# Second feed-forward product in three rounded-part products, in two halves of its inputs: a four-layer transformer stack on one Trainium2 core

## The reference, cut to what matters

```python
# each of blocks 0, 1, 2 (block 0 without the gate)
h = modulate(norm(x), cond)
q, k, v = h @ Wq + bq, h @ Wk + bk, h @ Wv + bv
x = x + gate1 * (softmax(q @ k.T * s) @ v @ Wp + bp)
h = modulate(norm(x), cond)
h = gelu(h @ W1 + b1, approximate=False)      # fc1: 256 -> 1024
x = x + gate2 * (h @ W2 + b2)                 # fc2: 1024 -> 256
# block 3: h2 = modulate(norm(h1)); return h2 + h1
```

## Time and profile before

| | |
|---|---|
| median of 3 runs | 1317.73 us (1311.64 to 1376.43) |
| profiled execution | 1313.94 us, of it 1312.2 us from first to last instruction |
| mean granted TensorE clock | 0.959 |
| TensorE matmuls busy | 1196.3 us |
| ScalarE busy | 777.1 us |
| VectorE busy | 780.6 us |
| GpSimd busy | 407.9 us |

### The profile page before, as it was taken

One profiled execution on the slowest core, in us unless ns is written; L12 is line 12 of the kernel. 1 busy time (PEld: TensorE's weight loads), 2 busy tenths in 40 slices (PEclk: granted clock), 3 DMA queues, 4 the chain that ended last, 5 costly groups with the idle time before them and its releaser, 6 DMA issues.

```text
span 1312.2 us, 19523 instructions
## 1 busy us (share of the span) xinstructions
PE 1196.3 (91%) x6484; PEld 725.4 (55%) x6484; DVE 780.6 (59%) x1587; ACT 777.1 (59%) x1363; POOL 407.9 (31%) x416
## 2 busy tenths in 40 slices
PE   4899998789989989999999989999999998999993
PEld 3668786445655545555555555556556555444432
DVE  4334245685685685574674654664755745787863
ACT  2563553267567468467566666575684674676771
POOL 2423255101143222332250251332322313434143
PEclk9999998799999999998999989999999999999987
DMA  7000000504304204312213331132133131242400
...
DMA packets 40852, 64.46 MB, mean 49 GB/s; under 512 B 11673, under 2 KB 26777, under 8 KB 40753
## 3 DMA queue, kind: packets, MB, share of 16 engines
...
## 4 chain that ended last, share of the span: by engine, by line
PE 67%; DVE 12%; issue 6%; SPq 6%; ACT 6%; DMA 2%; POOL 1%; ACTq 0%; POOLq 0%; DVEq 0%
PE ring L712 12%; PE ring L646 10%; PE AVB L659 9%; PE ring L572 8%; PE ring L574 7%; PE ring L573 7%; SPq L534 5%; PE ring L636 4%; DVE m L1049 4%; DVE stats L956 2%; PE ring L679 2%; PE ring L684 2%; ACT hT_h L762 1%; ACT L822 1%; ACT probs L822 1%
## 5 line engine op out<-in xcount | busy, mean ns | idle before, releaser
L1049 DVE TENSOR_REDUCE m<-ring 128x1 f32<-128x512 f32 x768 | 490.0, 684 | 181.7 <-PE ring L636 161.6
L822 ACT ACTIVATE probs<-ring 128x512 f32<-128x512 f32 x768 | 412.5, 612 | 265.2 <-PE ring L636 242.4
L646 PE MATMUL ring<-SQ,SK 49*128 49x512 f32 x768 | 292.4, 460 | 40.8 <-DVE cT L1056 15.0
L636 PE MATMUL ring<-SK,SQ 48*128 48x512 f32 x768 | 312.8, 477 | 16.6 <-ACT probs L822 13.5
L646 PEld LDWEIGHTS ring<-SQ,SK 49*128 49x128 f32 x768 | 131.7, 192 | 270.4 <-issue 90.3
L659 PE MATMUL AVB<-probs,V 128*32 128x512 f32 x1536 | 211.9, 620 | 0.8 <-issue 0.8
L712 PE MATMUL ring<-w_s,gT 128*128 128x256 f32 x768 | 176.8, 385 | 0.2
L636 PEld LDWEIGHTS ring<-SK,SQ 48*128 48x128 f32 x768 | 133.3, 193 | 55.5 <-ACT probs L822 40.4
L712 PEld LDWEIGHTS ring<-w_s,gT 128*128 128x128 f32 x768 | 143.3, 191 | 30.9 <-issue 12.2
L1158 POOL TENSOR_TENSOR tmp<-tmp,gates 128x256 f32<-128x256 f32 (+1 forms) x48 | 43.8, 914 | 253.0 <-DVE tmp L1097 217.7
L1126 POOL TENSOR_TENSOR postT_l<-full,postT_h 128x512 fp32r<-128x512 f32 x56 | 71.1, 1280 | 155.3 <-ACT postT_h L870 102.4
...
## 6 DMA issues: line engine op xcount, KB each, us to landing
...
gates<-gate_rows SPq DMA_DIRECT2D x12, 256.0 KB, 3.4
raw<-in_wqkv SPq DMA_DIRECT2D x9, 256.0 KB, 2.8
```

Of the source, the lines that this page charges most:

```text
L636: mm = pe.matmul(o[:, :], SQ[a % 4][r:r + KS, n // 2, c * P:(c + 1) * P], SK[a % 4][r:r + KS, n // 2, :], start=True, stop=True)
L646: mm = pe.matmul(o[:, :], SK[a % 4][r:r + KS + 1, n // 2, c * P:(c + 1) * P], SQ[a % 4][r:r + KS + 1, n // 2, :], start=True, stop=True)
L822: act.activation(probs[:, n % PROBS, :], bank(kind, a, i)[:, :], ACT.Exp, scale=SCALE[layer(unit_job(a))]).then_inc(done["scores"], 1)
L1049: nc.vector.tensor_reduce(m16[:, a % 2, col:col + 1], bank(kind, a, i)[:, :], AX_X, ALU.max, negate=True).then_inc(done["max"], 1)
```

## The change

- **fc2** becomes `product` of parts: `gT_h`, `gT_l` with `w2_h`, `w2_l`. `gelu` writes every hidden tile twice on ScalarE (`gT_f`, `gT_h`), and GpSimd subtracts (`gT_l`, in the same place as `gT_f`).
- To fit in memory `gT_h` and `gT_l` hold half of the hidden channels. So there is `fc2a` (the first 512 hidden channels) and `fc2` (the last 512), each as two steps of two token tiles; VectorE puts `fc2a` with the bias in `tmp` and adds `fc2` to it. The second gelu waits until `fc2a` has read the first half.
- The places: fc1 and gelu on ticks 8 and 13, `fc2a` on 11 and 12, `fc2` on 15 and on tick 0 of the next window, `v` for layers 2 and 3 on 9 and 10. In layer 0 `fc2a` comes after `pT0`, ahead of the second half of fc1.
- The second weight comes through `raw` in four pieces like the others. In layers 1 and 2 the nine pieces are split on every second tick from tick 8 of the layer's first window.
- `rowp` is loaded in a step of its own, `load_rows`, and the product with the gate rows is moved to `gatefix`, tick 4 of the next window. `wgate_s` is gone, its uses go through `wmod_s` and `qk`. The two-slot tile `full` is gone too: the full values lie where the remainder will be (`hT_f`, `postT_f`).

```diff
+T_FC1, T_FC2A, T_FC2 = (8, 13), (11, 12), (15, 16)
+T_V = (9, 10)
...
-        at[6] += [("v", j, 0), ("stack", UNITS * j, 0)]
-        at[7] += [("v", j, 1)]
+        at[6] += [("stack", UNITS * j, 0)]
+        at[T_V[0]] += [("v", j, 0)]
+        at[T_V[1]] += [("v", j, 1)]
...
-        for i, t in enumerate((8, 10)):
+        for i, t in enumerate(T_FC1):
             at[t] += [("fc1", j, m) for m in range(4 * i, 4 * i + 4)] + [("gelu", j, i)]
-        for t in range(TT):
-            at[12 + t] += [("fc2", j, t)]
+        for i in range(2):
+            at[T_FC2A[i]] += [("fc2a", j, i)]
+            at[T_FC2[i]] += [("fc2", j, i)]
     else:
+        at[4] += [("gatefix", j, 0)]
...
+def pieces_at(w):
+
+    first = TICKS * BATCH * layer(w)
+    if layer(w) == LAYERS - 1:
+        return [(first + 8, "wp", 0)]
+    order = [("wp", 0), ("w1", 0), ("w1", 1), ("w2", 0), ("w2", 1), ("w1", 2), ("w1", 3), ("w2", 2), ("w2", 3)]
+    return [(first + 8 + 2 * n, kind, i) for n, (kind, i) in enumerate(order)]
...
+        rest += [("split_" + kind, layer(w), i) for at, kind, i in pieces_at(w) if at == TICKS * w + t]
...
+        plan += [("load_" + kind, layer(w), i) for at, kind, i in pieces_at(w) if at == TICKS * w + t + 1]
         if t == 15 and batch(w) == 0:
-            plan.append(("load_wp", layer(w), 0))
...
+            plan.append(("load_rows", layer(w), 0))
...
-                elif kind == "fc2":
-                    pe.wait_ge(in_w2, 16 * (layer(a) + 1))
-                    for m in range(MT):
-                        if i == 0:
-                            pe.wait_ge(done["fc1"], nth("fc1", a, m))
-                        mm = pe.matmul(o[:, 0:DIM], gT[:, m, i * P:(i + 1) * P], w2_s[:, m, :],
-                                       start=(m == 0), stop=(m == MT - 1))
+                elif kind in ("fc2a", "fc2"):
+
+                    h = int(kind == "fc2")
+                    for t in range(2):
+                        tok = (2 * i + t) * P
+                        for m in range(MT // 2):
+                            if i == 0 and t == 0:
+                                pe.wait_ge(g_lo, (nth("gelu", a, h) - 1) * (MT // 2) + m + 1)
+                                pe.wait_ge(done["split_w2"], nth("split_w2", layer(a), 2 * h + m // 2))
+                            mm = product(o[:, t * DIM:(t + 1) * DIM], [x[:, m, tok:tok + P] for x in (gT_h, gT_l)],
+                                         [w[:, h * MT // 2 + m, :] for w in (w2_h, w2_l)], m == 0, m == MT // 2 - 1)
...
-                        act.activation(gT[:, m, :], bank("fc1", a, m)[:, :], ACT.Gelu,
-                                       bias=colv[:, layer(a), col:col + 1]).then_inc(done["fc1"], 1)
+                        for dst in (gT_f, gT_h):
+                            ins = act.activation(dst[:, m % (MT // 2), :], bank("fc1", a, m)[:, :], ACT.Gelu,
+                                                 bias=colv[:, layer(a), col:col + 1])
+                        ins.then_inc(done["fc1"], 1)
...
+                elif kind == "gelu":
+
+                    for m in range(MT // 2):
+                        pool.wait_ge(done["fc1"], nth("fc1", a, i * MT // 2 + m))
+                        nc.gpsimd.tensor_tensor(gT_l[:, m, :], gT_f[:, m, :], gT_h[:, m, :].bitcast(F32), ALU.subtract
+                                                ).then_inc(g_lo, 1)
...
-                elif kind == "gatecast" and layer(a) == LAYERS - 1:
+                elif kind == "gatefix":
```

More of the change, by code:

```diff
@@ L77, in post @@
 def post(j):
-    at = {t: [] for t in range(TICKS)}
+    at = {t: [] for t in range(2 * TICKS)}
     if multi(j):
@@ L113, in single_window @@
     j, n = w - 1, w + 1
-    hT2, fc1, fc2 = [], [], []
+    hT2, fc1, fc2a, fc2 = [], [], [], []
     if j >= 0:
@@ L117, in single_window @@
         fc1 = [("fc1", j, m) for m in range(MT)]
-        fc2 = [("fc2", j, t) for t in range(TT)]
+        fc2a = [("fc2a", j, t) for t in range(2)]
+        fc2 = [("fc2", j, t) for t in range(2)]
     else:
@@ L128, in single_window @@
     proj = [("proj", w, 0), ("proj", w, 1)]
-    steps += pT + fc1[half:]
+    steps += pT + fc2a + fc1[half:]
     if j >= 0:
@@ L166, in row_pairs @@
     return [s for n in (0, 2) for s in (scores[n], maxima[n + 1], scores[n + 1], maxima[n])]
+def pieces_at(w):
[4 more added lines that the diff above has]
+    return [(first + 8 + 2 * n, kind, i) for n, (kind, i) in enumerate(order)]
 def multi_window(w):
     before, after = post(w - 1), prep(w + 1)
+    if w > BATCH:
+        late = post(w - 2)
+        before = {t: late[t + TICKS] + before[t] for t in range(TICKS)}
     plan, last = [], layer(w) == LAYERS - 1
@@ L194, in multi_window @@
                 rest.append(("split_qkv", n, (t - 10) // 2))
-        if batch(w) == 1:
-            if t == 1:
-                rest.append(("split_wp", layer(w), 0))
-            if t in (3, 5, 7, 9) and not last:
-                rest.append(("split_w1", layer(w), (t - 3) // 2))
+        rest += [("split_" + kind, layer(w), i) for at, kind, i in pieces_at(w) if at == TICKS * w + t]
         v = t + LEAD
@@ L261 @@
 RINGED = ("hT1", "v", "qktok", "q", "k", "max", "shift", "oT1", "oT2", "proj", "hT2", "fc1",
-          "fc2", "gate", "modrow", "mod", "pT0", "av0", "scores", "scores0")
+          "fc2a", "fc2", "gate", "modrow", "mod", "pT0", "av0", "scores", "scores0")
 NTH, USE, USES = {}, {}, []
@@ L280 @@
 PIECES = [s for s in PLAN if s[0].startswith("split")]
-CUTS = [s for s in PLAN if s[0] in ("hT1", "hT2", "oT2", "av0")]
 def nth(kind, a, i=0):
@@ L376, in bank @@
             return ring[USE[(kind, a, i)] % RING]
-        kinds = sorted({s[0] for s in PLAN if not s[0].startswith("load") and s[0] not in ("stack", "store", "gelu", "gateout", "gatecast")})
+        kinds = sorted({s[0] for s in PLAN if not s[0].startswith("load") and s[0] not in ("stack", "store", "gelu", "gateout", "gatecast", "gatefix")})
         done = {k: sem("done_" + k) for k in kinds}
@@ L410, in cond_blocks_kernel @@
         final_dve = sem("final_dve")
-        first_in = [sem(f"first_in{n}") for n in range(sum(s[1] == 0 for s in PIECES))]
+        first_in = [sem(f"first_in{n}") for n in range(8)]
         def STACK_IN(u):
@@ L760, in _ @@
                     hi = postT_h if second else hT_h
-                    for dst in (whole(act, kind, a, i), hi[:, i, :]):
+                    full = postT_f if second else hT_f
+                    for dst in (full[:, i, :], hi[:, i, :]):
                         ins = act.activation(dst, bank(kind, a, i)[:, :], ACT.Identity,
@@ L1082, in _ @@
                                             ).then_inc(done[kind], 1)
-                elif kind in ("proj", "fc2"):
+                elif kind in ("proj", "fc2a", "fc2"):
                     l = layer(a)
```

158 lines of the change are left out of this document (83 added, 75 removed).

## The result

| | before | after |
|---|---|---|
| median, same set of runs | 1314.68 us (1311.36 to 1376.43) | 1381.07 us (1373.58 to 2077.08) |
| ratio | 1 | **1.0495**, 95% interval 1.0425 to 1.0565 |
| profiled execution, span | 1312.2 us | 1379.0 us |
| mean granted TensorE clock | 0.959 | 0.907 |

One execution of each kernel (2077 us and 1376 us) fell in a disturbed state of the chip and is left out of the ratio. The changed kernel is 5% slower; 1323 us was predicted, with a range up to 1348.

A forecast was written before the change was run, and what follows sets the result against it. TensorE, busy 1196.3 of 1312.2 us, was taken to bound the kernel. Terms +8.2 - 0.5 + 4.6 - 6.0 + 1.0 + 5.8 + 1.8 - 5.5 = +9.4 on 1313.9 gave 1323 us, range 1287 to 1348.

The forecast's parts named there:

- Layer 0: Layer 0's three jobs: faster fc2 gives -6.0 us; window 0's four weight splits add +1.
- 4 x 0.59 = 2.36 each, less 0.4: Layer 0, each of three jobs: four fc2 steps 0.59 us shorter, less 0.4 because fc2a closely follows gelu; -6.0 in all.
- Window 0's splits: Four weight splits in window 0, lying mostly beside TensorE's work: +1 us, bounds 0 and 4 x 1.3.
- The second writing: ScalarE writes eight gelu tiles instead of four, so exp and max product come 1.25 us later; bounds 0.0 and 2.1.
- 18 x 1.25 = 22.5: Gelu's delays at ticks 9 and 14; this falls away if TensorE does not wait, a rival forecasting 1289 us, chance 0.17.
- The clock: Rival: ticks 8 of windows 4 to 12 run partly at 1.2 GHz, +33 us, 1356 us; chance 0.13.
- v: Leaving ticks 6 and 7 gains 0; on ticks 9 and 10 adds 0.6 and 1.43 us, in windows 13 and 14 +4.6.
- fc2's rate: 24 matmuls of parts take 2.86 us against 3.65 a window step, -0.79; 35.5 us of TensorE work in all.
- no gain in fc2: Rival: matmuls of parts take 0.15 us instead of 0.119, so nothing of the 35.5 comes; 1358 us, chance 0.04.
- Weight pieces: Windows 4 and 8, tick 10: ScalarE waits for the next piece ahead of an exp, delaying TensorE; +3.9 and +1.9 us.
- rowp: Layer 3: tick 2 of window 13 falls from 10.45 to near 4.9 us, GpSimd losing its 46.66 us; -5.5.
- eight gelus at 0.69 us: Rival: gelu's eight writings take 0.69 us each instead of 0.58, +14 us, 1337 us; chance 0.06.

The follow-up runs named there:

- b_fc2first: Kernel before, float32 fc2 unchanged, with all four fc2 steps of layer-0 windows put ahead of the projection: ratio 1.0229 to the kernel before.
- a_best: Changed kernel with v on ticks 6 and 7, layer 0's fc2 after statistics, GpSimd rounding gelu from job 3, three splits and later weight pieces delayed: 1.0002 to kernel before.
- a_fc2f32: Changed kernel with fc2 again as one float32 matmul in place of three of parts, order and gelu's two writings kept: ratio 1.0711 to the kernel before.
- a_pieces: Changed kernel with the weight pieces after each layer's first one two ticks later: ratio 1.0547 to the kernel before.

## Why the prediction was wrong

**Layer 0, the main failure** (expected -6.0 + 1.0, measured +26.1). The step that failed is "4 x 0.59 = 2.36 each, less 0.4": it priced fc2 by its length and did not ask what fc2 covered. The waits that came in its place are 27 us longer in all (15.7 + 8.2 + 10.8 + 3.5 against 1.6 + 5.3 + 0.7 + 3.8), and the mean clock from 38 us to tick 2 of window 4 fell from 0.95 to 0.88. `b_fc2first` shows +2.3% from the order alone, and +25.0 us up to that tick; against it stand only 3 x 2.4 us of faster products. Window 0's splits took 5.2, the bound and not the 1.

**The second writing: right in place and mechanism, too small in size.** The term "18 x 1.25 = 22.5" was the wait alone; taking the writing away brought 2.5 to 3.0%, 33 to 39 us. A wait of 1.42 us stands where 1.6 was said. What the sum left out is the tick behind the wait: tick 9 +1.9 us and tick 15 +1.6 in window 10, all at a low clock.

**The clock: a rival with 0.13, and the nearest to what came.** Its price (+33) was put on ticks 8, behind ticks 6 and 7, and little of it came there: the nine ticks 8 of windows 4 to 12 cost 18.4 us more than nine times 8.27, against 15.5 before, which is +3. Tick 8 of window 10 went from 8.27 to 10.20, but that of window 9 from 13.66 to 8.70. The low clock came in ticks 7, 9 and 15 and ahead of window 4. The forecast's own sentence, that I am wrong if the mean clock falls clearly below 0.959, came true with 0.907. The trace speaks for the rule of the Trainium skill cited there (TensorE: Matmul & The Clock Gate, Part 1: The HAM clock gate), that activity releases the slow clock, in one respect: window 10 of `a_best` ran at 1.00, with v back in ticks 6 and 7 and the longer waits behind gelu gone. It does not show that activity is enough: the filled tick 14 had TensorE busy 5.78 of 5.80 us and a clock of 0.77.

**v: right.** Gain 0 in ticks 6 and 7: 10.83 against 11.08. Its new place was priced at 6 x (0.6 + 1.43) + 4.6 = 16.8 us; giving the old one back brought 0.6 to 1.0%, 8 to 13 us. Where these lie the prediction had wrong: in ticks 6 to 8, which grow by 1.07 us without v, and hardly in ticks 9 to 11 (0.29). Moved alone in the kernel before, v costs 2.6% or 36 us, more than the 8 x 2 x 1.43 = 23 us of its load; the clock fell with it to 0.936.

**fc2's rate: right for the matmuls, a little high for the step.** Tick 11 5.29 for 5.18, tick 0 6.24 for 6.22; a step gains 0.6 to 0.7 us where 0.79 was said, and `a_fc2f32` gives 23 to 28 us of the 35.5. The rival *no gain in fc2* is excluded.

**Weight pieces: ScalarE's wait is there, TensorE's is not.** ScalarE waits one tick later than predicted, in tick 11, 1.97 us in window 4:

```profile
347.65 0.63 ACT L761 ACTIVATE w_h<-raw 128x512 fp32r<-128x512 f32 x1 [1.97 <-DMA raw<-in_w]
```

The ticks are 2.6 and 1.3 us longer, for +3.9 and +1.9. But the prediction had TensorE wait there, and in tick 11 of window 4 it does not (length, TensorE busy, clock, DMA):

```profile
347.81:355.68 7.87, 7.87 (x42) 0.66 0.43 136
```

All of that tick's excess is the clock of 0.66, which was already 0.50 in tick 10; what part the late piece has in it is not shown. In window 8 TensorE waits 0.8 us. `a_pieces` shortened both ticks and not the total.

**rowp: the tick right to 0.1 us, the total wrong.** -5.5 in the tick; moved alone it brought nothing (1.0003, 0.9976 to 1.003). "What is late next there: nothing that I find" looked only at the tick's own chain.

**ScalarE's writings.** They stand 0.57 us apart in the kernel after (929.23 - 928.66 and the rows before it), not the 613 ns that the Trainium skill's figures gave (ScalarE: Activation LUTs, What ACT_TABLE_LOAD costs); the rival of eight gelus at 0.69 us is out.
